# ScalarE's order in the gated slots of a pipelined attention and feed-forward stack: table load and gated functions behind the copies out of PSUM

## What is computed

```
x = x + mamba(layernorm(x))                 # 16 sequences of 256 tokens, 128 features
x = x + stack(layernorm(x))

stack, 6 layers:
    x = attn_layer(shift_tokens(x), Wqkv, q_scale, k_scale, Wo) + x
    x = ffn_layer(shift_tokens(x), g, bln, W1, b1, W2, b2) + x

attn_layer: q, k, v = split(x @ Wqkv)       # 16 heads of 64
            q, k = rotary(l2norm(q) * qs), rotary(l2norm(k) * ksc)
            windowed softmax attention, window 32, looking one window back
            return out @ Wo
ffn_layer:  xn = layernorm(x) * g + bln
            a, gate = split(xn @ W1 + b1)   # 341 hidden columns each
            return a * gelu(gate) @ W2 + b2
```

## Time and profile before

| | before |
|---|---|
| median of three runs | 4343.53 us (4338.90 to 4343.79) |
| profiled execution | 4346.03 us, span 4344.2 us |
| TensorE busy | 3711.1 us, 85% of the span, 60112 products |
| VectorE busy | 3134.8 us, 72% |
| ScalarE busy | 2690.0 us, 62%, 4972 instructions |
| GpSimd busy | 2388.6 us, 55% |
| L684 and L719, the two table loads | 96 each, 1.283 us each, 123.2 us each |
| L676, the gated functions | 144, 0.69 us each, 99 us in all |
| six layers | from 670 us to the end; about 75 us for each group of eight slots |

### The profile page before, as it was taken

One profiled execution on the slowest core, in us unless ns is written; L12 is line 12 of the kernel. 1 busy time (PEld: TensorE's weight loads), 2 busy tenths in 40 slices (PEclk: granted clock), 3 DMA queues, 4 the chain that ended last, 5 costly groups with the idle time before them and its releaser, 6 DMA issues.

```text
span 4344.2 us, 145197 instructions
## 1 busy us (share of the span) xinstructions
PE 3711.1 (85%) x60112; PEld 2254.7 (52%) x60128; DVE 3134.8 (72%) x3609; ACT 2690.0 (62%) x4972; POOL 2388.6 (55%) x1813
## 2 busy tenths in 40 slices
PE   5677667898888889988888898988888898988888
PEld 2222223555555555555555555555555555555554
DVE  4899996767766676766766676667766676767774
ACT  4455444666666666666666666666666666666665
POOL 0455554655555555555555555555555555555551
PEclk9899897999999999999999999999999999999999
DMA  2000000000010100110000111000110001110001
GB/s 68 0 0 0 0 0 18 28 28 23 28 42 29 32 28 28 33 42 29 29 28 24 42 33 33 29 24 28 47 31 26 28 28 42 33 30 26 28 28 34
DMA packets 64403, 119.93 MB, mean 28 GB/s; under 512 B 18196, under 2 KB 35986, under 8 KB 63634
## 3 DMA queue, kind: packets, MB, share of 16 engines
q1 hardware_dynamic: 63762, 110.70, 8.7%
HBM read 20.50 MB, written 2.10 MB: 5 GB/s over the span
## 4 chain that ended last, share of the span: by engine, by line
PE 50%; DVE 12%; ACT 12%; issue 11%; POOL 0%; ACTq 0%; DMA 0%; DVEq 0%; POOLq 0%; SPq 0%
PE qk L1125 12%; PE ob L1183 9%; PE sc L1210 6%; PE trb L997 5%; PE vob L1191 4%; PE sc L1159 3%; DVE ssq L890 3%; PE vob L1131 3%; PE sc L1217 3%; ACT L719 3%; DVE mx L897 3%; ACT arena L617 2%; PE ob L997 2%; DVE arena L885 2%; ACT arena L631 2%
## 5 line engine op out<-in xcount | busy, mean ns | idle before, releaser
L498 POOL TENSOR_TENSOR arena<-arena 128x1024 f32<-128x1024 f32 x384 | 907.5, 2363 | 701.8 <-DVE arena L885 651.6
L505 POOL TENSOR_TENSOR arena<-arena,rnorm 128x512 f32<-128x512 f32 x768 | 794.1, 1055 | 781.8 <-ACT rnorm L624 781.8
L1125 PE MATMUL qk<-wqkv,xs 128*128 128x512 f32 x1536 | 820.3, 661 | 268.8 <-ACT xs L662 261.4
L884 DVE TENSOR_TENSOR arena<-qk,tab_q 128x1024 f32<-128x1024 f32 x192 | 235.2, 1225 | 956.9 <-ACT arena L617 952.3
L631 ACT ACTIVATE arena<-trb 128x512 f32<-128x512 f32 x768 | 464.3, 604 | 544.5 <-PE trb L997 544.5
L617 ACT ACTIVATE arena<-qk 128x512 f32<-128x512 f32 x768 | 445.7, 594 | 294.2 <-PE qk L1125 291.8
L1125 PEld LDWEIGHTS qk<-wqkv,xs 128*128 128x128 f32 x1536 | 305.1, 205 | 618.0 <-issue 541.9
L997 PE MATMUL trb<-ident,arena 128*128 128x128 f32 x3072 | 483.6, 280 | 7.3 <-ACT arena L631 5.9
L483 POOL TENSOR_TENSOR arena<-arena 128x512 f32<-128x512 f32 x256 | 300.4, 1183 | 344.0 <-DVE arena L856 328.6
L890 DVE TENSOR_REDUCE ssq<-arena 128x16 f32<-128x1024 f32 x384 | 464.1, 1209 | 0.0
L512 POOL TENSOR_TENSOR arena<-arena,rinv 128x512 f32<-128x512 f32 x384 | 393.0, 1045 | 65.9 <-DVE rinv L907 65.9
(11 more groups left out here) (139 smaller groups left out, 5972.0 us busy)
## 6 DMA issues: line engine op xcount, KB each, us to landing
arena<-arena SPq DMA_DIRECT2D x192, 384.0 KB, 3.2
arena<-arena SPq DMA_DIRECT2D x192, 64.0 KB, 3.0
wqkv<-in_L_ffn_Wqkv SPq DMA_DIRECT2D x18, 512.0 KB, 3.8
wo<-in_L_ffn_Wo SPq DMA_DIRECT2D x6, 512.0 KB, 4.0
arena<-in_L_attn_x SPq DMA_DIRECT2D x8, 256.0 KB, 2.9
out<-arena SPq DMA_DIRECT2D x8, 256.0 KB, 2.2
w<-in_L_ffn_W SPq DMA_DIRECT2D x6, 341.0 KB, 2.9
arena<-in_sel SPq DMA_DIRECT2D x1, 1024.0 KB, 5.0
```

The source lines that it names most:

```text
L498: nc.gpsimd.tensor_tensor(ts[c * 2 + j], tu[:, 0], tu[:, 1], ALU.add).then_inc(summed[0], 1)
L505: nc.gpsimd.tensor_tensor(part, part, rnorm[j][:, 8 * h:8 * h + 8].unsqueeze(2).to_broadcast([P, 8, HEAD]), ALU.mult) \
L1125: MM(QK[:, 512 * h:512 * h + 512], lhsT=xs[u][:, c * P:(c + 1) * P], rhs=wqkv[:, col:col + 512], start=True, stop=True) \
```

## The change

Only the order of ScalarE's `layer_slot` changes. The block with the gelu table load and the gated functions moves from behind the squares to behind the slot's copies out of PSUM, right in front of the load of the Exp and Ln table. Nothing else moves; in slots without gated functions the order is the same.

```diff
                 if unit:
                     squares(*unit)
                 up0, up1 = group_at(l, k, LAG_UP[0]), group_at(l, k, LAG_UP[1])
-                if up0 or up1:
-                    act_e.preload_act_table(ACT.Gelu)
-                if up0:
-                    gelu(*up0, 0, 0, 0)
-                    gelu(*up0, 1, 1, 512)
-                if up1:
-                    gelu(*up1, 2, 2, 0)
                 at_ = unit_at(l, k, LAG_TURN)
                 if at_:
                     turned(*at_, 0)
...
                 if value and k % 2:
                     v_evac(value[0], value[3:], value[2])
+                if up0 or up1:
+                    act_e.preload_act_table(ACT.Gelu)
+                if up0:
+                    gelu(*up0, 0, 0, 0)
+                    gelu(*up0, 1, 1, 512)
+                if up1:
+                    gelu(*up1, 2, 2, 0)
                 if up0 or up1:
                     act_e.preload_act_table_set(EXP_LN_SET)
```

## The result

The changed kernel takes 4560.19 us (median, 4557.19 to 4573.85) against 4343.66: ratio 1.0507, interval 1.0484 to 1.053. That is 216 us more, where 258 were forecast (4602, range 4545 to 4650). The profiled execution took 4557.19 us with a span of 4555.3, 211.1 more than before.

The account below looks back on a forecast made before the run. The prediction took the end of ScalarE's gated slots, waited for by TensorE and VectorE, as the bound. It added 117 + 90 + 44 + 7 = 258 us to the median of 4343.53, giving 4602 us, range 4545 to 4650.

Parts of the forecast that it names:

- What bounds the kernel: End of ScalarE's gated slots: practically all 96 table loads, 123 us in all, lie on the path that sets the end.
- (a): Both gated slots: copies out of TRB, OB and VOB move forward; gain 0, at most 14 us.
- (b): First gated slot: load and two gated functions add 2.60 us in front of the xs copies, 117 us in all.
- (c): Second gated slot: load and function add 2.00 us ahead of norms, staging and the next squares, 90 us in all.
- the rival in which the slot is absorbed: Second gated slot: slack hides its longer tail, so only the first slot counts; 4512 us, chance 0.08.
- (d): TensorE's four projection products behind the longer xs wait all run at half clock, adding 44 us.
- clock mixture unchanged: Products behind the longer xs wait: as many cases as before come out fast; 4558 us, chance 0.10.
- (e): Last three groups: scores wait 3.5 and about 2.9 us for the gated functions, 7 us in all.
- The drain of a table load: Both gated slots: each load holds the next function 1.36 us longer, 122 us more; 4724 us, chance 0.03.

Follow-up runs that it names:

- two pairs: Kernel before with two more pairs of do-nothing table loads (5.14 us) in the first gated slot, otherwise old order: 4655.6 us, ratio 1.0722.
- the pair kernel without a move: Kernel before with one more pair of do-nothing table loads (2.57 us) in the first gated slot, otherwise old order: 4500.72 us, ratio 1.0368.
- the moved one: Kernel before with only the first gated slot's gelu load and two functions moved behind the copies: 4498.53 us, ratio 1.036.
- the pair there: Kernel before with one more pair of do-nothing table loads (2.57 us) in the second gated slot only, otherwise old order: 4493.16 us, ratio 1.0343.
- the pair in both slots: Kernel before with one more pair of do-nothing table loads (2.57 us) in both gated slots, otherwise old order: 4616.28 us, ratio 1.0622.
- early staging: Next sequence's xs copies directly behind the VOB copy: 4142.27 us in the kernel before; in the changed kernel, ahead of gelu's load and functions, 4275.48 us.

## Why the prediction held, point by point

*What bounds the kernel.* Right: L719's 3% meant that what stands beside it is paid one to one. The shortest stretches grow by 2.57, 2.00, 2.51 and, with two pairs, 5.15 us (42.16 against 37.01): the tail's growth each time, within 0.06 us. The period from one first gated slot to the next grew by 2.35 + 2.12 = 4.5 us on average; the forecast had 5 to 6.

*(a) The forward move is worth nothing.* Right for the first slot, where it is shown from both sides: the pair kernel without a move equals the moved one within 2.2 us, and taking the block away from the old place changed nothing (ratio 0.9999, both slots). For the second slot only the latter is shown; the pair there cost 58 us more than the move beyond the difference of their tails, and TensorE's busy time was 70 us higher; what part the earlier copies have in that stays open.

*(b) First gated slot,* 2.60 us: measured 2.57 in front of the xs copies, wait 5.96 us in the median against the 6.0 forecast.

*(c) Second gated slot,* 2.00 us: measured 1.99, with the forecast 1.1 us wait for the gated function ahead of the scores. The rival in which the slot is absorbed is refuted by 67 us for that slot alone and by its shortest stretch.

*(d) The clock.* This term was mis-sized: 44 us forecast, about -3 measured. Its mechanism was there: behind the 6 us waits all 45 groups were slow. Two things in its working failed. First, "if a wait of 6.0 us makes all wholly slow, 0.97 x 45" took the stretches of 38.15 us for the price (in the trace of before 18 groups took 3.77 or 3.78 us, not 19, and their mean stretch is 38.19); only 24 of the 45 groups of the changed kernel were wholly slow, and the A stretches grew by 0.36 us beyond their tail, 16 us. Second, it kept the slow groups behind the 1.9 us waits as they were, and they fell from 16 to 5 of 44: B stretches grew by 0.45 us less than their tail, -20 us. The case "clock mixture unchanged" (4558) came out nearest in time, though the mixture did change; two changes cancelled. That they did was luck: with the pair in both slots 24 us remained above the tails. The measured time lies in the range because the lower end allowed for a clock term of nothing. TensorE's busy time rose by 20 us even so; that this did not lengthen the stretches is measured, and why is not known. The first slot alone has +29 in its stretches, two thirds of the 44, so the term is real for that half of the edit.

*(e) The end.* The two waits came as forecast: 3.38 and 2.93 us ahead of the scores behind the last staged group's gated slots, against 3.5 and 2.9.

```profile
4460.25 0.59 PE L1153 MATMUL sc<-mask,ident 128*128 128x512 bf16 x2 [3.38 <-ACT xnT L676]
...
4477.03 0.59 PE L1153 MATMUL sc<-mask,ident 128*128 128x512 bf16 x2 [2.93 <-ACT hid_last L676]
```

Behind the last staging the kernel grew by 9.1 us instead of 7, with the first slot alone by 11.9 and with the second alone by 0.5. So these two waits are not all that the end is made of; the rest is not traced here.

*The drain of a table load.* No gap: L712 at 2627.32 and the function at 2628.61 are 1.29 us apart. The Trainium skill ("ScalarE: Activation LUTs", "What ACT_TABLE_LOAD costs") has the load's 1283 ns as measured here; its further 1.38 us did not appear: in the changed kernel 190 of the 192 loads are followed by the next ScalarE instruction 1.29 or 1.30 us after their start.

## What to carry to other kernels

Before moving work on an engine that is busy 62% of the time, look not at its share but at what stands last in its stage: ScalarE's tail was waited for by TensorE in one slot and by VectorE in the other, while the slot's middle held 2 to 3 us of free time. Put what others wait for (here two copies of 0.4 us, and the next slot's squares) ahead of table loads and of work read two slots later: that gave 4.6 and another 1.4 points. Shortening TensorE's waits here was worth more than their length, 182 us in the stretches for 102 us of waits, since the clock came back with it.

## What was not expected of the hardware

How often TensorE's products behind one and the same wait ran at the half clock depended on what lay elsewhere in the program. Behind the 1.9 us waits it was 16 of 44 before, and between 5 and 39 in kernels that leave these waits alone; behind waits of 3.4 us it was 32 of 45 before, and 27 and 42 in the two kernels that change the second gated slot alone. Behind waits of 1.5 us it was none of 85 in the kernel before with early staging and 1 of 85 in the changed one with it; behind waits of 5.8 us and more it was all. The stretch between two waits is all that the edits have in common (it grew by 2.0, 2.57 or 5.14 us), but no simple relation to it shows: 1.99 us more in the second slot lowered the count to 5, 2.57 us more there raised it to 26. What decides it stays open. In the seven kernels with longer tails the growth of the stretches lay between 30 us under and 60 us over the tails themselves, and no row of the trace of before would have told where in it.
